# One core, graph attention: GpSimd makes the mask of the outside neighbours for 5 of 16 key tiles

## What is computed

```python
seq = (x @ W_seq).reshape(N, H, DH)               # N = 2048, H = 16, DH = 32
score1 = einsum('nhd,d->hn', seq, a1)
score2 = einsum('nhd,d->hn', seq, a2)
scores = leaky_relu(score1[:, :, None] + score2[:, None, :], 0.2)
scores = scores + (1.0 - adj)[None] * -65500.0
attn   = softmax(scores, axis=-1)
hidden = einsum('hij,jhd->ihd', attn, seq)
```

## Time and profile before

| | us |
|---|---|
| median of 3 runs (2367.80 to 2375.20) | 2375.08 |
| time of the profiled execution | 2367.94 |
| its span, first to last instruction | 2366.2 |
| busy in the span: PE | 2115.8 |
| busy in the span: DVE | 1550.8 |
| busy in the span: ACT | 1091.3 |
| busy in the span: POOL | 554.4 |

### The profile page before, as it was taken

One profiled execution on the slowest core, in us unless ns is written; L12 is line 12 of the kernel. 1 busy time (PEld: TensorE's weight loads), 2 busy tenths in 40 slices (PEclk: granted clock), 3 DMA queues, 4 the chain that ended last, 5 costly groups with the idle time before them and its releaser, 6 DMA issues. The chain is left out here.

```text
span 2366.2 us, 43008 instructions
## 1 busy us (share of the span) xinstructions
PE 2115.8 (89%) x18260; PEld 1241.5 (52%) x18260; DVE 1550.8 (66%) x2500; ACT 1091.3 (46%) x1070; POOL 554.4 (23%) x412
## 2 busy tenths in 40 slices
PE   6799999999996899879999999998695499999997
PEld 3444444444442444344444444443244488888887
DVE  7768888888885767758768777775144644444442
ACT  5667888888881233303444444445221222222221
POOL 0000000000001012323555555546430222222211
PEclk9899999999998999959999999999895699999999
DMA  7411111212115112343021031000230444444431
GB/s 252 146 57 43 71 55 59 75 43 71 54 41 185 39 45 89 136 104 85 19 64 45 24 81 31 15 22 12 99 125 18 152 116 116 116 112 115 112 68 23
DMA packets 81134, 185.27 MB, mean 78 GB/s; under 512 B 8208, under 2 KB 17424, under 8 KB 75408
## 3 DMA queue, kind: packets, MB, share of 16 engines
q1 hardware_dynamic: 71984, 161.55, 20.9%
q0 software_dynamic: 8960, 20.98, 4.7%
HBM read 137.81 MB, written 40.37 MB: 75 GB/s over the span
## 5 line engine op out<-in xcount | busy, mean ns | idle before, releaser
L450 ACT ACTIVATE m_step<-m_ub,gat_bias 128x2048 bf16<-128x2048 f32 x256 | 493.8, 1992 | 120.5 <-DVE m_mask L527 107.3
L1146 DVE TENSOR_REDUCE t_rm<-t_m 128x1 f32<-128x512 f32 (+3 forms) x640 | 373.0, 605 | 159.0 <-PE t_m L1202 95.0
L1088 ACT ACTIVATE t_E<-t_s 128x1024 f32<-128x1024 f32 (+3 forms) x320 | 277.7, 894 | 389.7 <-PE t_s L1219 195.1
L527 DVE TENSOR_TENSOR m_mask<-m_step,gat_adjT 128x2048 bf16<-128x2048 bf16 x256 | 306.8, 1222 | 84.7 <-ACT m_step L450 72.8
L1067 POOL TENSOR_TENSOR t_total<-t_E 128x1024 f32<-128x1024 f32 (+2 forms) x160 | 308.3, 1939 | 185.6 <-PE t_d L1246 185.6
L1202 PE MATMUL t_m<-t_K,t_Q 96*128 96x512 f32 (+3 forms) x640 | 276.9, 455 | 50.4 <-DVE t_rm L1146 29.2
L1202 PEld LDWEIGHTS t_m<-t_K,t_Q 96*128 96x128 f32 x640 | 125.4, 200 | 208.2 <-DVE t_rm L1146 143.5
L567 PE MATMUL m_bd<-m_mask,m_S 128*32 128x512 bf16 x3072 | 212.0, 380 | 8.0 <-DVE m_mask L527 7.8
L567 PE MATMUL m_bd<-gat_adjT,m_S 128*32 128x512 bf16 x3072 | 211.6, 380 | 4.8 <-PE m_dn L567 4.8
L567 PE MATMUL m_bd<-m_mask,m_neg 128*32 128x512 bf16 x3072 | 211.8, 380 | 0.0
L1219 PE MATMUL t_s<-t_Q,t_K 97*128 97x512 f32 (+3 forms) x640 | 208.4, 401 | 0.5 <-ACT t_E L1088 0.5
(11 more groups left out here) (299 smaller groups left out, 3379.2 us busy)
## 6 DMA issues: line engine op xcount, KB each, us to landing
a_adj<-in_adj SPq DMA_DIRECT2D x16, 1024.0 KB, 4.9
m_ub<-scratch_uac SPq DMA_DIRECT2D x16, 1024.0 KB, 4.7
e_w1r<-in_L_ffn_w SPq DMA_DIRECT2D x8, 2048.0 KB
e_w2r<-in_L_ffn_w SPq DMA_DIRECT2D x8, 2048.0 KB, 9.0
t_Q<-scratch_parts SPq DMA_DIRECT2D x48, 256.0 KB, 4.9
t_K<-scratch_parts SPq DMA_DIRECT2D x9, 1024.0 KB, 15.1
m_scale<-scratch_uac SPq DMA_DIRECT2D x32, 256.0 KB
scratch_parts<-o_hi SPq DMA_DIRECT2D x32, 256.0 KB, 2.1
```

The costliest lines, as they stand in the source:

```text
L450: act.activation(step[n % RELUS][:, :], ub[h % 2][:, :], ACT.Relu, bias=bias[:, j, h:h + 1], scale=BIG).then_inc(step_ready, 1)
L527: dve.tensor_tensor(mask[n % MASKS][:, :], step[n % RELUS][:, :], adjT[:, j, :], ALU.min).then_inc(mask_ready, 1)
L1088: act.activation(E[n % 3][:, two, off:BANK], ps_s[:, two, off:BANK], ACT.Exp, scale=SCALE).then_inc(exp_done[z], 1)
L1146: dve.tensor_reduce(rm[:, h, t, ch:ch + 1], ps_m[i % 2][:, 0:w], AX, ALU.max).then_inc(entry_read, 1)
```

## The change

For tiles 1, 4, 7, 10 and 13 of each head (OUTER) POOL computes adjacency minus mask, the mask of the outside neighbours, 128x2048 bf16 from two bf16 inputs in SBUF. Its output goes to one of two buffers laid in memory that is idle at the time (a part of `hT` for heads 0 to 3, of `seq` after that), in 16 runs of 128. For these tiles PE leaves out the 12 matmuls against the adjacency and the 12 of `neg`, and runs 12 of S against the outside mask instead, two tiles later (LAG = 2), ahead of that tile's wait for its own mask. DVE may overwrite the mask of such a tile only once POOL has read it too.

```diff
+OUTER, LAG = (1, 4, 7, 10, 13), 2
...
+        late, used = hT[:, :, 3, :].bitcast(BF16), seq[:, :, 0:P].bitcast(BF16)
+        outer = lambda h, k: (late if h < 4 else used)[:, :, k % 2 * P:(k % 2 + 1) * P]
+        number = lambda h, j: h * len(OUTER) + OUTER.index(j)
+        outer_ready, outer_free = sem("m_outer"), sem("m_outer_free")
...
+                for h in range(H):
+                    for j in OUTER:
+                        n, k = h * T + j, number(h, j)
+                        pool.wait_ge(mask_ready, n + 1)
+                        if k >= 2:
+                            pool.wait_ge(outer_free, k - 1)
+                        pool.tensor_tensor(outer(h, k), adjT[:, j, :].rearrange("p (t q) -> p t q", t=T),
+                                           mask[n % MASKS][:, :].rearrange("p (t q) -> p t q", t=T),
+                                           ALU.subtract).then_inc(outer_ready, 1)
...
                     if n >= MASKS:
                         dve.wait_ge(mask_free, n - MASKS + 1)
+                        before = divmod(n - MASKS, T)
+                        if before[1] in OUTER:
+                            dve.wait_ge(outer_ready, number(*before) + 1)
...
+                def outer_products(h, j, down):
+                    k = number(h, j)
+                    pe.wait_ge(outer_ready, k + 1)
+                    for s in range(SPLITS):
+                        for c in range(4):
+                            mm = pe.matmul(down[c * TILE:(c + 1) * TILE, :], S[h % 2][:, j, s, DH:2 * DH],
+                                           outer(h, k)[:, 4 * c:4 * c + 4, :], start=False, stop=False)
+                    mm.then_inc(outer_free, 1)
...
-                        for s in range(SPLITS):
-                            for c in range(4):
-                                spread(down, S[r][:, j, s, DH:2 * DH], adjT[:, j, :], c,
-                                       start=(first and s == 0), stop=False)
+                        if j not in OUTER:
+                            for s in range(SPLITS):
+                                for c in range(4):
+                                    spread(down, S[r][:, j, s, DH:2 * DH], adjT[:, j, :], c,
+                                           start=(first and s == 0), stop=False)
+                        if j - LAG in OUTER:
+                            outer_products(h, j - LAG, down)
...
-                        for s in range(SPLITS):
-                            for c in range(4):
-                                spread(down, neg[r][:, j, s, :], moving, c, start=False, stop=(last and s == 2))
+                        if j not in OUTER:
+                            for s in range(SPLITS):
+                                for c in range(4):
+                                    spread(down, neg[r][:, j, s, :], moving, c, start=False, stop=(last and s == 2))
```

## The result

The changed kernel takes 2551.93 us (median of 4 runs, 2549.68 to 2556.39) against 2372.43 of the kernel before (median of 4): a ratio of 1.0764, 95% interval 1.0743 to 1.0785. It is 180 us slower. The forecast was 2590, range 2515 to 2635. The profiled execution has a span of 2554.4 us, 188.2 more than before.

What follows compares the result with a forecast made beforehand. The loop of DVE and ACT was taken to bound each 37.0 us head. POOL's standstills add 14 x 14.2 + 12.7 + 13.3 = 224.8, less 5: 220 on 2367.9 gives 2588, said as 2590 us, range 2515 to 2635.

Steps and rivals of the forecast that it cites:

- a loop of DVE and ACT: In each head, DVE and ACT set the 37.0 us; removing 3.4 us of PE's matmuls is worth nothing.
- The standstill of 16-bit inputs: DVE masks with two SBUF inputs take turns with POOL's bf16 subtraction, as seen in f32, saving only 0.13 us.
- The first rival: No standstill for 16-bit inputs: POOL works beside DVE, a head stays 37.0 us, 2360 to 2368; chance 0.06.
- The order: Who goes first at each tile: POOL at tiles 1 and 4, DVE's next operation at 7, 10 and 13.
- The pieces: Time added per head at tiles 1, 4, 7, 10, 13: 3.85, 2.84, 0.30, 4.32, 2.90, sum 14.2 us.
- POOL's operation: Length of one 128x2048 bf16 subtraction on POOL: 4.58 us, from f32 rows, bounds 3.78 to 5.0.
- The 5 us off: Guessed gain from DVE's waits for PE outside the steady heads, taken off the sum of 224.8 us.
- PE's clock: Rival: pauses lower PE's clock, some 45 us a head, still under 51; low all through, 65 us, 2810; chance 0.03.
- The signs: Profile after: subtraction about 4.6 us, some masks 4 to 5.5, longer ACT waits, heads 51 apart, PE under two thirds busy.

Runs made afterwards that it cites:

- PE's part alone: Against the changed kernel, POOL's work and all added waits dropped; PE still runs 28 matmuls in place of 40 for the five tiles: 2363.95 us, ratio 0.9976.
- POOL's fill: Against the changed kernel, POOL's subtraction replaced by two constant fills of the same buffer that read nothing, all added waits kept: 2368.06 us.
- tile 10 alone: Against the changed kernel, POOL's subtraction kept only for tile 10 of each head, 16 in place of 80: 2456.68 us, ratio 1.0362 to the kernel before.
- the third buffer: Kernel before plus a third buffer for ACT's step, with POOL's subtraction for tile 7 alone: 2426.93 us; with POOL waiting for mask 8: 2361.17 us.

## Why the prediction was right, point by point

- **What binds.** That PE's 36.07 us a head hide a loop of DVE and ACT was read from the waits and from a sum of starts that gave 37.0. PE's part alone (2364, a head unchanged) shows it.
- **The standstill of 16-bit inputs**, the one step taken over and not seen, holds: masks of 4 to 4.6 us beside POOL's subtraction, 1.22 beside POOL's fill. The first rival would have given 2360 to 2368. One reading against that rival was wrong: the earlier trace rows show two forms of DVE operation standing still, not three. The third, a TENSOR_SCALAR that took 2.98 us instead of 0.43, stands in the trace at 758.45 and not in the rows.
- **The order** came out as worked: POOL first at tiles 1 and 4, DVE first at 7, 10 and 13.
- **The pieces.** With 4.07 in place of 4.58 (0.51 less in four pieces, and 0.30 at tile 7), the forecast's pieces would be 3.34, 2.33, 0, 3.81 and 2.39, in sum 11.87. The timeline gives 3.34 (9.13, tile 1 to 3, against 5.79), 2.32 (10.89, tile 3 to 7, against 8.57), 0.01, 3.75 and 2.37, in sum 11.8: a head of 48.79.
- **The term that was mis-sized** is POOL's operation, "I take 4.58, as the row nearest in kind". It took 4.07. At 2.3 us a head and 16 heads that is 37 of the 38 us by which 2590 missed 2552. That only 1 us is left is luck, since the times behind the stage differ by several us from run to run. The wrong inference was from memsets: a fill shows that POOL writes at one pace for 2 and 4 bytes, and says nothing about reading; with bf16 inputs the subtraction is a tenth shorter.
- **The 5 us off** for PE's waits at the start, a guess, were not seen: with 4.07 in place of 4.58 the forecast's sum, before the 5 are taken off, is 187 us (14 x 11.87, some 10.2 for the first head and 11.0 for the last), and the last `take` comes 186.7 us later than before. DVE waited for PE 18.0 us in the stage of after, 10.4 before. With PE's part alone 3.8 us did come back.
- **PE's clock.** As forecast it fell in part (0.93 over that head, in which PE was busy 37.3 us and not the 45 of the rival) and cost nothing in heads of 49 us, not even with PE's 60 matmuls back in them (48.80). The forecast's sum holds only for heads with such slack: with tile 10 alone the clock did cost.
- **The signs.** Masks of 4 us and more, ACT's longer waits and the last product of `divide` (0.69 as before) came as forecast; heads are 48.8 us apart and not 51. That POOL's group has a mean of 4.63 us, near the 4.58, is chance: in three of its five rows POOL's wait for DVE is in it. "PE under two thirds busy" failed: it was busy 37.33 of 48.79 us, 77%, since part of its matmuls ran at the lower clock.

## What to carry to other kernels

Before work is moved to POOL, look at what DVE does beside it. Here a POOL operation of 4.07 us that reads SBUF held up a DVE operation with two SBUF inputs until its own end (masks of 4 to 4.6 us instead of 1.22), so its price was nearly its own duration and not a share of it. A single input is no safe sign: the cast stood still as well (4.47 us instead of 0.71), while the reciprocal kept its 3.35. Under that reciprocal POOL cost nothing as long as mask 8 was ahead of it. To be sure of that, POOL has to wait for the beginning of that stretch and not merely for its data: with the third buffer a head took 40.96 us without that wait and 36.52 with it. And before matmuls are saved on an engine that is 97% busy, add up the loop of the others: here it was as long as the whole head.

## What the runs showed that was not expected

- POOL's two-input operation depends on the inputs' type and on nothing else that was varied: 4.05 us from bf16, 4.50 from f32, for 2048 columns.
- A cast with a single SBUF input is held up by POOL's reading (4.47 us for 0.71) and by its writing too (1.22); the masks, with two inputs, by its reading only.
- A pause of 4.84 us of PE was followed by some 5 us at the lower clock in one head and 2.6 in the next, even though dense work followed at once, so with little slack a standstill of 3.8 us cost 6.1.
